# Half-step order of a joined scan-and-read stage, with the scan's normalised rows written by ScalarE

## The chip, the cores and the metric

The kernel runs on one core of one Trainium2 chip. The metric is the device time of one execution in microseconds. The kernel before has a median of 6312.4 us over three runs (6304.77 to 6313.58). In the text, a time is in us unless marked ns.

## The reference, cut to what matters

A network of four layers acts on x of shape 4 x 512 x 64 x 64 in float32. The change touches only the first, a test-time-training linear layer with 8 heads of 64 channels. The 4096 tokens of an image go through a scan in chunks of 16:

```python
def step(carry, inp):
    W1c, b1c = carry
    xq, xk, xv, et = inp
    Z1 = xk @ W1c + b1c
    grad = _ln_l2_bwd(Z1, xv - xk, g, bb)
    Attn1 = jnp.tril(xq @ xk.swapaxes(-1, -2))
    b1_bar = b1c - jnp.tril(et) @ grad
    Z1_bar = xq @ W1c - et * Attn1 @ grad + b1_bar
    last_eta = et[..., -1, :, None]
    W1n = W1c - (last_eta * xk).swapaxes(-1, -2) @ grad
    b1n = b1c - (last_eta * grad).sum(-2, keepdims=True)
    return ((W1n, b1n), xq + _ln(Z1_bar, g, bb, EPS_IN))
...
return _ln(out, post_w, post_b, EPS_IN) @ o_w.T
```

`_ln_l2_bwd` normalises Z1 (the normalised rows are `xh`) and returns the gradient of a squared error. The state W1, b1 goes from chunk to chunk, so the scan is one long chain. The outputs (Z1_bar, its norm, the post norm and the last projection) are off that chain.

## The kernel before

The program runs one stage after another: channel statistics, the projection of queries, keys and values, then the function `scan_and_read`, then a Fourier layer, a gate and a second Fourier layer. Only `scan_and_read` is changed. It joins two jobs.

The scan has 256 steps, one for each chunk of 16 tokens, of all four images at once. The images are in two groups of two (`g` 0 and 1). For each group a step is: `project_k` (TensorE: the bias sum and 16 small matmuls with the state into `ps_z`), `spread` (ScalarE: squares with their sums, then the root), `gradients` (VectorE: `zg`, the reciprocal `rstd`, the normalised rows `xh`, `t_row`, `tx`, `cx`, `core`, and `step`; GpSimd makes the rates, `b_step`, `b_sum` and `stored`), `update` (TensorE: the state in PSUM, `ps_w`), and `state_out` (ScalarE: the state from PSUM to SBUF for the next `project_k`). In the first step of each 8 the state is copied to `w_snap` in place of `w_sb`, and is kept there for the reads.

The read works on tiles of 128 tokens of one image, one tile for each two steps, through a pipeline: a tile is turned and weighted in slot KQ (4 slots after its own), summed in OUT (5), normalised in NORM (6), projected in PROJ (7) and leaves in LEAVE (8). One slot is two steps: an even one (`at.odd` 0) and an odd one. I call such a pair of steps a period; there are 128.

Each engine has its own queue, and its order of work is written out by hand in a function `body`. A step is cut into half steps: work of group 0, tile work, work of group 1, tile work. TensorE's order is `project_k(0)`, tile work, `update(1)` of the step before, tile work, `project_k(1)`, tile work, `update(0)`, tile work. In the even step its tile work is `tile_bias_and_state`, `tile_outputs_turn`, `tile_weighted` and the first of four `tile_project` parts; in the odd step `tile_query_turn`, `tile_project` 1, 2 and 3, `tile_weights` and `turn_keys`. ScalarE's order in the even step is `spread(0)`, `keys_out`, `normed`, `state_out(1)`, `outputs_turned`, `spread(1)`, `squares`, `state_out(0)`; in the odd step `spread(0)`, `head_roots`, `query_turned`, `output_squares`, `state_out(1)`, `spread(1)`, `output_root`, `state_out(0)`. VectorE's order in the even step is `gradients(0)`, `leave`, `gradients(1)`, `head_sums`, `outputs`, `moments`; in the odd step `gradients(0)`, `head_norms`, `variance`, `gradients(1)`, `shift_of`, `weights`. Waits on semaphores, counted by steps and tiles, tie the queues together; SyncE issues the transfers in its own order, the tile's rows of x (`x_sb`, line 1671) in the odd step of slot PROJ.

Of the kernel before, what the change touches and what calls it, by code (L numbers as in the profile page):

```python
# [13 lines left out]
P = 128  # L14
# [1385 lines left out]
def scan_and_read(nc, T, d, x_in, rec, q_in, grad, s_snap, x_out, chan_stats):  # L1400
# [14 lines left out]
    with ExitStack() as ctx:  # L1415
# [60 lines left out]
        x_sb = sb("x_in", [P, CT, P])  # L1476
# [50 lines left out]
        xh_sb = sig("xh_sb")  # L1527
# [9 lines left out]
        state_sb = sig("state_sb")  # L1537

# [3 lines left out]
        x_loaded = one("x_loaded", 16)  # L1542
# [63 lines left out]
        def state_of(g, at):  # L1606

            return w_snap[g][at.p] if at.c == 0 else w_sb[g]

        @block.sync  # L1610
        def _(sp):
# [36 lines left out]
            def body(at, scan):  # L1648
# [12 lines left out]
                if at.odd:  # L1661
                    tile = at.tile(LEAVE)
                    if tile:
                        t, b, sc, _ = tile
                        sp.wait_ge(y_done.sem, y_done.at(t, 1))
                        sp.dma_start(o_view[b, :, :, bass.ds(sc * P, P)], y_sb[b % 2][:]).then_inc(y_gone[b % 2].sem, 16)
                    tile = at.tile(PROJ)
                    if tile:
                        t, b, sc, _ = tile

                        sp.dma_start(x_sb[:], x_view[b, :, :, bass.ds(sc * P, P)]).then_inc(x_loaded.sem, 16)
# [47 lines left out]
        def _(pool):  # L1719
# [29 lines left out]
            def gained(tile):  # L1749
                t, b, sc, _ = tile  # L1750
                pool.wait_ge(zn_sb.sem, zn_sb.at(t, 1))
                pool.wait_ge(o_done.sem, o_done.at(t, 0))
                v.tensor_tensor(zgain[:], zn[:], read_gain[:].rearrange("p (h e) -> p h e", h=NH), ALU.mult).then_inc(zgain_sb.sem, 1)
# [7 lines left out]
            def body(at, scan):  # L1761
                if scan:
                    gradients(at, 0)
                if not at.odd and at.tile(NORM):
                    gained(at.tile(NORM))
# [8 lines left out]
        def _(act):  # L1774
            a = nc.scalar

# [41 lines left out]
            def squares(tile):  # L1818
                t, b, sc, _ = tile

                act.wait_ge(zn_sb.sem, zn_sb.at(t, 0))
                for n in range(2):
                    act.wait_ge(out_ps.sem, out_ps.at(t, n + 1))
                    a.copy(zo[:].rearrange("p (a n) e -> p a n e", n=2)[:, :, n], ps_out[n][:, :, 0:HD]).then_inc(zo_sb.sem, 1)
                act.wait_ge(hsq_sb.sem, hsq_sb.at(t, 0))
                act.wait_ge(zo_sb.sem, zo_sb.at(t, 2))
                a.activation(zsq[:], zo[:], ACT.Square).then_inc(zsq_sb.sem, 1)
# [25 lines left out]
            def body(at, scan):  # L1853
                kq, out, norm, proj = (at.tile(n) for n in (KQ, OUT, NORM, PROJ))
                following = Place(at.v, at.p, at.c + 1) if at.c < 7 else Place(at.v + at.p, 1 - at.p, 0)
                if scan:
                    spread(0, at.s)
                if not at.odd and (scan or at.slot == 0) and not (isinstance(at.s, int) and at.s == 0):

                    keys_out(at.v * 8 + at.slot + B - 1, at.p if at.c == 0 else 1 - at.p, (at.c // 2 - 1) % B)  # L1860
                if at.odd:
                    if out:
                        head_roots(out)
                    if kq:
                        query_turned(kq)
                    if norm:
                        output_squares(norm)
                elif proj:
                    normed(proj)
                if scan:  # L1870
                    state_out(1, at)
                if not at.odd and proj:
                    outputs_turned(proj)
                if scan:
                    spread(1, at.s)
                if at.odd:
                    if norm:
                        output_root(norm)
                elif out:
                    squares(out)  # L1880
                if scan:
                    state_out(0, following)
# [4 lines left out]
        def _(dve):  # L1887
# [34 lines left out]
            def gradients(at, g):  # L1922
# [12 lines left out]
                v.tensor_tensor(xh[g][:], z, wide(rstd[g][:]), ALU.mult).then_inc(xh_sb[g].sem, 1)  # L1935
# [4 lines left out]
                dve.wait_ge(xh_sb[g].sem, xh_sb[g].at(s, 1))  # L1940
# [18 lines left out]
            def leave(tile):  # L1959
# [3 lines left out]
                dve.wait_ge(x_loaded.sem, x_loaded.at(t, 16))  # L1963
                dve.wait_ge(y_gone[q].sem, y_gone[q].at(sc * 2 + b // 2, 0))
                dve.wait_ge(stats_sb.sem, stats_sb.at(t, 0))
                for n in range(CT):
                    done = v.scalar_tensor_tensor(y_sb[q][:, n], ps_y[:, n], T.wo_bias[:, n:n + 1], x_sb[:, n], ALU.add, ALU.add)  # L1967
# [9 lines left out]
            def outputs(tile):  # L1977
                t, b, sc, _ = tile
                dve.wait_ge(zgain_sb.sem, zgain_sb.at(t, 1))
# [3 lines left out]
                v.scalar_tensor_tensor(o_sb[:], zgain[:].rearrange("p h e -> p (h e)"), 1.0, qb[:].rearrange("p h e -> p (h e)"),  # L1983
# [28 lines left out]
            def head_norms(tile):  # L2012
# [5 lines left out]
                dve.wait_ge(zgain_sb.sem, zgain_sb.at(t, 0))  # L2018
                v.tensor_tensor(zn[:], zo[:], hrstd[:].unsqueeze(2).broadcast_to([P, NH, HD]), ALU.mult).then_inc(zn_sb.sem, 1)
# [9 lines left out]
            def body(at, scan):  # L2029
# [3 lines left out]
                if at.odd:  # L2033
                    if out:
                        head_norms(out)
                    if norm:
                        variance(norm)
                elif gone:
                    leave(gone)
                if scan:  # L2040
                    gradients(at, 1)
                if at.odd:
                    if norm:
                        shift_of(norm)
                    if kq:
                        weights(kq)
                else:
                    if out:
                        head_sums(out)
                    if norm:  # L2050
                        outputs(norm)
                    if gone:
                        moments(gone)
# [7 lines left out]
        def _(pe):  # L2061
# [47 lines left out]
            def tile_bias_and_state(tile):  # L2109
# [3 lines left out]
                pe.wait_ge(weigh_sb.sem, weigh_sb.at(t, 2))  # L2113
                out = [ps_out[n][:, :, 0:HD] for n in range(2)]
# [65 lines left out]
            def body(at, scan):  # L2180
# [6 lines left out]
                if at.odd:  # L2187
                    if kq:
                        tile_query_turn(kq, proj)
                    if proj:  # L2190
                        tile_project(proj, 1)
                elif out:
                    tile_bias_and_state(out)
                if update_last:
                    update(1, before)
                if at.odd:
                    if proj:
                        tile_project(proj, 2)
                elif proj:
                    tile_outputs_turn(proj)  # L2200
# [5 lines left out]
                elif out:  # L2206
                    tile_weighted(out)
                if scan:
                    update(0, at)
                if at.odd:  # L2210
                    if proj:
                        tile_project(proj, 3)
# [4 lines left out]
                elif proj:  # L2217
                    tile_project(proj, 0)
# [298 lines left out]
```

## Time and profile before

| | |
|---|---|
| median of the runs | 6312.4 us |
| the profiled execution's own time | 6306.89 us |
| its span | 6304.9 us |
| `scan_and_read`, first to last scan step in the trace | about 1720 to 4380 us |
| PE, DVE, ACT, POOL busy over the span | 87%, 65%, 36%, 38% |
| mean granted TensorE clock | 0.899 of full speed |

PE is TensorE, DVE is VectorE, ACT is ScalarE, POOL is GpSimd. PEclk 1.00 is 2.4 GHz and 0.50 is 1.2 GHz. In a timeline row the figures are the start and the duration in us of a run of equal instructions; `xN` counts them; a bracket gives the idle time of the engine before it and what ended it.

### The profile page before, as it was taken

What the parts mean: (1) busy time and instruction counts of PE and PEld (TensorE: products, weight loads), DVE (VectorE), ACT (ScalarE), POOL (GpSimd) and SP (SyncE); (2) the same over time, 40 slices, a digit from 0 to 9 for tenths busy, and PEclk for the clock granted to TensorE, in tenths of its full rate; (3) what the DMA queues carried; (4) which work ended last, traced back from release to release, by engine and by line L of the source; (5) the groups of instructions that cost most, each with busy time, mean ns of one, the idle gap of its engine ahead of it and who ended that gap; (6) DMA issues with size and microseconds to landing.
All of it is one profiled execution on the core that took longest, in us unless ns stands there. A gap on an engine that the chain in (4) does not pass through costs nothing. (4 is left out here: it accounts for less than half of the span.)

```text
span 6304.9 us, 141772 instructions
## 1 busy us (share of the span) xinstructions
PE 5494.0 (87%) x41532; PEld 3914.7 (62%) x41532; DVE 4074.0 (65%) x14538; ACT 2270.6 (36%) x6131; POOL 2390.9 (38%) x3910
## 2 busy tenths in 40 slices
PE   1799999999578889888888888888699999599999
PEld 0344444444267777777777777777566666377777
DVE  5566666566477777777777777777566666544444
ACT  0111111111155545555555555554233333233333
POOL 0244444444255544545545544544121222222222
PEclk9899999999778888888788878888899999799999
DMA  6233333333334444444444444444222211122221
GB/s 244 72 126 124 121 133 118 126 119 126 121 103 122 117 121 121 119 115 119 117 116 121 121 118 115 118 119 126 85 87 87 86 73 58 68 96 86 86 86 69
DMA packets 823322, 694.07 MB, mean 110 GB/s; under 512 B 357224, under 2 KB 758000, under 8 KB 811664
## 3 DMA queue, kind: packets, MB, share of 16 engines
q1 hardware_dynamic: 732304, 542.54, 28.9%
q10 hardware_dynamic: 90240, 142.75, 6.1%
q8 instruction: 293, 4.80, 0.3%
q14 instruction: 485, 3.97, 0.2%
HBM read 402.96 MB, written 282.20 MB: 109 GB/s over the span
## 5 line engine op out<-in xcount | busy, mean ns | idle before, releaser
L1390 PE MATMUL proj_ps<-proj_w_sb,proj_h 128*128 128x512 f32 x3072 | 1345.4, 596 | 0.0
L1390 PEld LDWEIGHTS proj_ps<-proj_w_sb,proj_h 128*128 128x128 f32 x3072 | 577.5, 190 | 742.9 <-issue 716.1
L2173 PE MATMUL scan_ps_y<-scan_o_t,proj_wo_sb 128*128 128x128 f32 x4096 | 631.0, 302 | 15.5 <-DVE scan_y L1967 14.8
L1312 DVE SCALAR_TENSOR_TENSOR proj_lin<-proj_ps,proj_rstd,proj_wbias_sb 128x512 f32<-128x512 f32 x384 | 284.4, 747 | 547.1 <-PE proj_ps L1390 546.1
L2173 PEld LDWEIGHTS scan_ps_y<-scan_o_t,proj_wo_sb 128*128 128x128 f32 x4096 | 547.1, 208 | 65.7 <-issue 26.0
L1736 POOL TENSOR_TENSOR scan_b_step<-scan_core,scan_rate_last 128x128 f32<-128x128 f32 x512 | 318.5, 622 | 640.0 <-DVE scan_core L1951 640.0
L2105 PE MATMUL scan_ps_w<-scan_step,scan_record 64*128 64x128 f32 x4088 | 430.0, 339 | 22.1 <-DVE scan_step L1956 21.8
L1787 ACT ACTIVATE scan_square<-scan_ps_z 128x64 f32<-128x64 f32 x1024 | 219.0, 219 | 569.5 <-PE scan_ps_z L2093 567.2
L1260 POOL TENSOR_TENSOR proj_by_cos<-proj_lin,proj_rope 128x512 f32<-128x512 f32 x256 | 340.1, 1338 | 138.9 <-DVE proj_lin L1312 109.4
L1266 POOL TENSOR_TENSOR proj_gk<-proj_rec,proj_gain_sb 128x256 f32<-128x256 f32 x256 | 181.1, 728 | 554.9 <-DVE proj_rec L1333 554.9
L2105 PEld LDWEIGHTS scan_ps_w<-scan_step,scan_record 64*128 64x128 f32 x4088 | 336.8, 230 | 56.5 <-DVE scan_step L1956 30.7
L266 POOL TENSOR_TENSOR fourier_spec<-fourier_prod 128x448 f32<-128x448 f32 (+1 forms) x80 | 93.1, 1164 | 704.9 <-DVE fourier_prod L410 704.8
L1780 ACT COPY scan_state_w<-scan_ps_w 128x512 f32<-128x512 f32 x448 | 259.2, 579 | 278.9 <-PE scan_ps_w L2105 273.7
L2117 PE MATMUL scan_ps_out<-scan_b_in,scan_ones 64*128 64x256 f32 x512 | 118.7, 549 | 276.4 <-DVE scan_weigh L2026 254.9
L2128 PE MATMUL scan_ps_out<-scan_grad_in,scan_weigh 128*128 128x64 f32 x2048 | 347.2, 340 | 0.0
L1728 POOL TENSOR_TENSOR scan_rate<-scan_rstd,scan_record 128x2 f32<-128x2 f32 x512 | 100.4, 196 | 649.0 <-DVE scan_rstd L1933 647.1
L2128 PEld LDWEIGHTS scan_ps_out<-scan_grad_in,scan_weigh 128*128 128x128 f32 x2048 | 328.0, 251 | 18.0 <-issue 14.1
L487 PE MATMUL fourier_psD<-fourier_mats,fourier_turned 128*128 128x128 f32 x2148 | 295.9, 282 | 42.1 <-DVE fourier_spec L389 39.6
L281 ACT COPY fourier_turned<-fourier_psT 128x512 f32<-128x512 f32 (+3 forms) x289 | 156.5, 550 | 488.7 <-PE fourier_psT L480 488.7
L487 PEld LDWEIGHTS fourier_psD<-fourier_mats,fourier_turned 128*128 128x128 f32 x2148 | 277.5, 197 | 86.6 <-issue 50.7
L706 POOL TENSOR_TENSOR fourier_spec<-fourier_prod 128x448 f32<-128x448 f32 (+1 forms) x80 | 86.4, 1080 | 618.8 <-DVE fourier_prod L799 618.8
L2087 PE MATMUL scan_ps_z<-scan_b_sum,scan_heads 128*32 128x128 f32 x4096 | 258.4, 331 | 46.2 <-issue 45.0
(287 smaller groups left out, 12263.8 us busy)
## 6 DMA issues: line engine op xcount, KB each, us to landing
scan_record<-records SPq DMA_DIRECT2D x1032, 98.0 KB
records<-proj_rec ACTq DMA_DIRECT2D x128, 784.0 KB, 3.6
scan_k_in<-records SPq DMA_DIRECT2D x266, 128.0 KB
spectra<-fourier_spec SPq DMA_DIRECT2D x16, 2112.0 KB, 6.4
fourier_spec<-spectra SPq DMA_DIRECT2D x16, 2112.0 KB, 8.2
stats_x<-x SPq DMA_DIRECT2D x16, 2048.0 KB, 7.8
proj_h<-x SPq DMA_DIRECT2D x32, 1024.0 KB, 7.1
queries<-proj_q ACTq DMA_DIRECT2D x128, 256.0 KB, 3.7
```

The costliest lines, as they stand in the source:

```text
L487: done = pe.matmul(psD[t % 2][:, col:col + P], turned[t % 2][:, j * P:(j + 1) * P], mat, start=True, stop=True)
L1260: g_.tensor_tensor(by_cos[q][:, n].rearrange("p (a e) -> p a e", e=32), lin[q][:, n].rearrange("p (a e) -> p a e", e=32), cos, ALU.mult).t ...
L1266: g_.tensor_tensor(by_parity(gk[q][:], n), keys(j, n), by_parity(T.gain[:], n), ALU.mult)
L1312: v.scalar_tensor_tensor(lin[q][:, n], ps[q][n][:], rstd[k][:, j:j + 1], T.wbias[:, n], ALU.mult, ALU.add).then_inc(lin_sb.sem, 1)
L1390: last = pe.matmul(ps[j % 2][n][:], h[k][:, ct, j * P:(j + 1) * P], T.w[:, n, ct], start=ct == 0, stop=ct == CT - 1)
L1736: v.tensor_tensor(b_step[g][:], core[g][:], rate_last[g][:, :, 2:3].broadcast_to([P, PB, HD]), ALU.mult).then_inc(b_step_sb[g].sem, 1)
L1780: a.copy(state_of(g, at)[:].rearrange("p r b a e -> p r (b a e)"), ps_w[:, :, g].rearrange("p r b a e -> p r (b a e)")).then_inc(state_sb[ ...
L1787: a.activation(square[:, g, b], ps_z[g][:, b * HD:(b + 1) * HD], ACT.Square, accum_out=ssq[g][:, b:b + 1]).then_inc(ssq_sb[g].sem, 1)
L2087: pe.matmul(ps_z[g][32 * a:32 * a + 32, 0:F], heads[:, 32 * a:32 * a + 32], b_sum[g][at.c % RING][:].rearrange("p b e -> p (b e)"), start= ...
L2105: done = pe.matmul(ps_w[:, r, g, b].rearrange("p a e -> p (a e)"), record[g][at.ring][rows, b, 0:2 * HD], step[g][rows, b].rearrange("p a ...
L2128: done = pe.matmul(ps_out[n][:, a, 0:HD], weigh[n][:, a], grad_sb[b % 2][:, 2 * a + n], start=False, stop=True, skip_group_check=True)
L2173: done = pe.matmul(ps_y[:, n], T.wo[:, ct, n * P:(n + 1) * P], o_t[:, ct], start=ct == 0, stop=ct == CT - 1)
```

## The change

- VectorE no longer makes `xh`. `spread` on ScalarE, after the root, waits for VectorE's reciprocal and makes `xh` with two activations (one for each image) that copy `ps_z` with a scale taken from `rstd`. VectorE waits for both before `tx`.
- The order of tile work changes on TensorE, ScalarE, VectorE and GpSimd.
- `w_snap[1]` is no longer written from PSUM but by a copy from `w_sb[1]` in the second step of each 8 (`keep_state`).
- The gain is multiplied before the norm of the heads, not after it; the number of operations stays.
- `x_sb` has two buffers, and its load is issued one slot earlier.

```diff
 state_of:   return w_snap[0][at.p] if g == 0 and at.c == 0 else w_sb[g]

 ScalarE
+            def keep_state(at, out):
+                sc = at.v * 2 + at.p
+                if out:
+                    act.wait_ge(out_ps.sem, out_ps.at(out[0], 2))
+                act.wait_ge(state_sb[1].sem, state_sb[1].at(at.s, 0))
+                a.copy(w_snap[1][at.p][:]..., w_sb[1][:]...).then_inc(kept_sb.sem, 1)
+                act.wait_ge(kept_sb.sem, kept_sb.at(sc, 1))
 spread:
                 a.activation(std[g][:], ssq[g][:], ACT.Sqrt, bias=eps[:]).then_inc(std_sb[g].sem, 1)
+                act.wait_ge(cx_sb[g].sem, cx_sb[g].at(s, 0))
+                act.wait_ge(rstd_sb[g].sem, rstd_sb[g].at(s, 1))
+                for b in range(PB):
+                    a.activation(xh[g][:, b], ps_z[g][:, b * HD:(b + 1) * HD], ACT.Copy, scale=rstd[g][:, b:b + 1]).then_inc(xh_sb[g].sem, 1)
 body, after:
                 spread(0); if even: keys_out
                 odd:  keep_state (second step of 8), outputs_out(out), output_squares(norm)
                 even: head_roots(norm)
                 state_out(1)
                 odd:  query_turned(kq)          even: normed(proj)
                 spread(1)
                 odd:  head_squares(out), output_root(norm)     even: outputs_turned(proj)
                 state_out(0)
...
 VectorE, gradients:
-                v.tensor_tensor(xh[g][:], z, wide(rstd[g][:]), ALU.mult).then_inc(xh_sb[g].sem, 1)
-                dve.wait_ge(xh_sb[g].sem, xh_sb[g].at(s, 1))
+                dve.wait_ge(xh_sb[g].sem, xh_sb[g].at(s, PB))
 body, after:
                 gradients(0)
                 odd:  variance(norm), moments(gone)            even: head_norms(norm), leave(gone)
                 gradients(1)
                 odd:  shift_of(norm), head_sums(out), weights(kq)     even: outputs(norm)
...
 TensorE, body, after:
                 project_k(0)
                 odd:  tile_query_turn(kq), tile_project(proj, 0)
                 update(1) of the step before
                 odd:  tile_project(proj, 1)                    even: tile_project(gone, 3)
                 project_k(1)
                 odd:  tile_weights(kq)                         even: tile_outputs_turn(proj), tile_bias_and_state(out)
                 update(0)
                 odd:  tile_project(proj, 2), turn_keys         even: tile_weighted(out)
...
 GpSimd: gained(out) in the odd step, between the groups; it reads zo
 SyncE:
-                    tile = at.tile(PROJ)
-                        sp.dma_start(x_sb[:], x_view[...]).then_inc(x_loaded.sem, 16)
+                    tile = at.tile(NORM)
+                        sp.dma_start(x_sb[b % 2][:], x_view[...]).then_inc(x_loaded[b % 2].sem, 16)
```

## Rows read from the trace of the kernel before

**Rows 1.** Busy us of each engine, 2200 to 4200 us, granted clock.
```profile
2200.00:4200.00 2000.00, 1746.67 (x21124) 1529.95 (x21122) 1536.97 (x7553) 1030.80 (x3394) 1004.05 (x2078) 0.81 0.45 118
```
**Rows 2.** Groups by line, 2200 to 4200 us: busy us, mean ns, idle before.
```profile
L2087 PE MATMUL scan_ps_z<-scan_b_sum,scan_heads 128*32 128x128 f32 x3016 | 189.7, 331 | 36.2 <-issue 36.2
L1935 DVE TENSOR_TENSOR scan_xh<-scan_ps_z,scan_rstd 128x128 f32<-128x128 f32 x378 | 110.1, 291 | 13.0
L1967 DVE SCALAR_TENSOR_TENSOR scan_y<-scan_ps_y,proj_wo_bias_sb,scan_x_in 128x128 f32<-128x128 f32 x377 | 106.1, 344 | 140.4 <-DMA scan_x_in<-x 139.7
```
**Rows 3.** Two stretches of 2 us, columns as in rows 1.
```profile
3026.00:3028.00 2.00, 0.40 (x4) 0.16 (x2) 1.75 (x13) 0.43 (x1) 0.60 (x3) 1.00 0.35 80
...
3032.00:3034.00 2.00, 2.00 (x18) 1.77 (x17) 0.00 (x0) 0.82 (x2) 0.00 (x0) 0.50 0.56 162
```
**Rows 4.** Timeline of VectorE, odd step from 3002.64, even step from 3011.33.
```profile
3000.26 0.68 DVE L1993 TENSOR_REDUCE scan_hsq<-scan_zsq 128x8 f32<-128x512 f32 x1
...
3001.86 0.87 DVE L1975 BATCH_NORM_STATS2 scan_stats<-scan_y 128x128 f32 x4
3002.64 0.27 DVE L1930 TENSOR_TENSOR scan_zg<-scan_ps_z,scan_gain 128x128 f32<-128x128 f32 x1
3002.84 0.15 DVE L1933 RECIPROCAL scan_rstd<-scan_std 128x2 f32<-128x2 f32 x1
3003.02 0.29 DVE L1935 TENSOR_TENSOR scan_xh<-scan_ps_z,scan_rstd 128x128 f32<-128x128 f32 x1
3003.23 0.47 DVE L1938 SCALAR_TENSOR_TENSOR scan_t_row<-scan_zg,scan_rstd,scan_record 128x64 f32<-128x64 f32 x2
...
3005.25 0.20 DVE L2016 RECIPROCAL scan_hrstd<-scan_hstd 128x8 f32<-128x8 f32 x1
...
3006.09 0.41 DVE L1999 TENSOR_TENSOR scan_ovar<-scan_nmean 128x1 f32<-128x1 f32 x1
...
3011.33 0.28 DVE L1930 TENSOR_TENSOR scan_zg<-scan_ps_z,scan_gain 128x128 f32<-128x128 f32 x1
```
**Rows 5.** Timeline of TensorE in the same even step, clock 1.00.
```profile
3011.47 0.70 PE L2117 MATMUL scan_ps_out<-scan_b_in,scan_ones 64*128 64x256 f32 x4 [2.90 <-DVE scan_weigh L2026]
...
3012.84 0.67 PE L2105 MATMUL scan_ps_w<-scan_step,scan_record 64*128 64x128 f32 x8
3013.44 0.66 PE L2137 MATMUL scan_ps_turn<-proj_ident_sb,scan_on 128*128 128x128 f32 x4
3014.02 0.42 PE L2087 MATMUL scan_ps_z<-scan_b_sum,scan_heads 128*32 128x128 f32 x8
3014.26 0.41 PE L2093 MATMUL scan_ps_z<-scan_state_w,scan_k_t 128*32 128x64 f32 x16
3014.60 2.00 PE L2128 MATMUL scan_ps_out<-scan_grad_in,scan_weigh 128*128 128x64 f32 x16
3016.53 0.72 PE L2105 MATMUL scan_ps_w<-scan_step,scan_record 64*128 64x128 f32 x8
```
**Rows 6.** Timeline of ScalarE around the same even step.
```profile
3009.18 0.30 ACT L1790 ACTIVATE scan_std<-scan_ssq,scan_eps 128x2 f32<-128x2 f32 x1
3009.39 1.24 ACT L1797 COPY scan_k_t<-scan_ps_turn 64x512 f32<-64x512 f32 x2
3010.65 0.81 ACT L1810 ACTIVATE scan_on<-scan_o,scan_oshift,scan_orstd 128x512 f32<-128x512 f32 x1
3013.55 0.58 ACT L1780 COPY scan_state_w<-scan_ps_w 128x512 f32<-128x512 f32 x1 [2.09 <-PE scan_ps_w L2105]
...
3014.74 0.22 ACT L1787 ACTIVATE scan_square<-scan_ps_z 128x64 f32<-128x64 f32 x1
```
**Rows 7.** Timeline of TensorE in an even step at clock 0.50.
```profile
3030.29 0.93 PE L2117 MATMUL scan_ps_out<-scan_b_in,scan_ones 64*128 64x256 f32 x4 [0.59 <-DVE scan_weigh L2026]
...
3032.61 1.18 PE L2105 MATMUL scan_ps_w<-scan_step,scan_record 64*128 64x128 f32 x8
...
3035.77 3.68 PE L2128 MATMUL scan_ps_out<-scan_grad_in,scan_weigh 128*128 128x64 f32 x16
```

More of the change, by code:

```diff
@@ L1537, in scan_and_read @@
         state_sb = sig("state_sb")
+        kept_sb = one("kept_sb")
         k_loaded = one("k_loaded", 32)
@@ L1541, in scan_and_read @@
         grad_in = [one(f"grad_loaded{q}", 48) for q in range(2)]
-        x_loaded = one("x_loaded", 16)
+        x_loaded = [one(f"x_loaded{q}", 16) for q in range(2)]
         y_gone = [one(f"y_gone{q}", 16) for q in range(2)]
@@ L1763, in body @@
                     gradients(at, 0)
-                if not at.odd and at.tile(NORM):
-                    gained(at.tile(NORM))
+                if at.odd and at.tile(OUT):
+                    gained(at.tile(OUT))
                 if scan:
@@ L1861, in body @@
                 if at.odd:
+                    if scan and at.c == 1:
+                        keep_state(at, out)
                     if out:
-                        head_roots(out)
+                        outputs_out(out)
+                    if norm:
+                        output_squares(norm)
+                elif norm:
+                    head_roots(norm)
+                if scan:
+                    state_out(1, at)
+                if at.odd:
                     if kq:
                         query_turned(kq)
-                    if norm:
-                        output_squares(norm)
                 elif proj:
@@ L1870, in body @@
                 if scan:
[L1871 to L1874, printed above, removed]
                     spread(1, at.s)
                 if at.odd:
+                    if out:
+                        head_squares(out)
                     if norm:
                         output_root(norm)
-                elif out:
-                    squares(out)
+                elif proj:
+                    outputs_turned(proj)
                 if scan:
@@ L2033, in body @@
                 if at.odd:
-                    if out:
-                        head_norms(out)
                     if norm:
                         variance(norm)
-                elif gone:
-                    leave(gone)
+                    if gone:
+                        moments(gone)
+                else:
+                    if norm:
+                        head_norms(norm)
+                    if gone:
+                        leave(gone)
                 if scan:
@@ L2044, in body @@
                         shift_of(norm)
+                    if out:
+                        head_sums(out)
                     if kq:
                         weights(kq)
[L2047 to L2053, printed above, removed]
+                elif norm:
+                    outputs(norm)
             loop(dve, body)
@@ L2190, in body @@
                     if proj:
-                        tile_project(proj, 1)
-                elif out:
-                    tile_bias_and_state(out)
+                        tile_project(proj, 0)
                 if update_last:
@@ L2197, in body @@
                     if proj:
-                        tile_project(proj, 2)
-                elif proj:
-                    tile_outputs_turn(proj)
+                        tile_project(proj, 1)
+                elif gone:
+                    tile_project(gone, 3)
                 if scan:
@@ L2205, in body @@
                         tile_weights(kq)
-                elif out:
-                    tile_weighted(out)
+                else:
+                    if proj:
+                        tile_outputs_turn(proj)
+                    if out:
+                        tile_bias_and_state(out)
                 if scan:
@@ L2216, in body @@
                         turn_keys(at.v * 8 + at.slot + B)
-                elif proj:
-                    tile_project(proj, 0)
+                elif out:
+                    tile_weighted(out)
             loop(pe, body)
```

40 lines of the change are left out of this document (24 added, 16 removed).

## The prediction

> **What bounds the kernel now.** I read the page's slices first: the joined stage holds some 2660 of 6305 us and is the only one that the change touches. Then the busy time in its steady part, 2200 to 4200 us [rows 1]: TensorE works 1747 of 2000 us, VectorE 1537, ScalarE 1031, GpSimd 1004, at a mean granted clock of 0.81. The `xh` instruction ran 378 times there [rows 2], four times for each pair of steps, so there were 94.5 periods and one lasts 21.16 us. Per period TensorE idles 2000 minus 1747, over 94.5, which is 2.68 us.
>
> The clock is the second half of the story. With only the two levels 1.00 and 0.50, a mean of 0.81 means 38% of the time at 1.2 GHz, 8.0 us of each period. The stretches show where: in 3026 to 3028 TensorE worked 0.40 of 2 us at 1.00, and in 3032 to 3034 it worked all the time and had 0.50 [rows 3]. So a wait of TensorE of some 3 us costs itself and then makes the work behind it slow.
>
> Third, the timelines show what TensorE waits for. It idled 2.90 us in the even step for VectorE's `weights` [rows 5], the last thing that VectorE does in the odd step. VectorE starts its next `zg` at 3011.33, 8.69 us after the odd step's `zg` at 3002.64, without a gap between [rows 4]. So in the odd half VectorE is the bound, and in the even half TensorE's queue is, the more so at 1.2 GHz: bias and state take 1.37 us at the high clock (3011.47 to 3012.84, [rows 5]) and 2.32 at the low one (3030.29 to 3032.61, [rows 7]).
>
> **The change part by part.**
>
> *`xh` on ScalarE.* VectorE saves 0.21 us a time (3003.02 to 3003.23, [rows 4]). But `tx` needs `xh`. No row of before shows an activation of this form, so I bound it. From below: the square of the same 128x64 shape, without scale, lasts 0.22 [rows 6]. From above: the root, 0.30, whose next instruction starts 0.21 later, plus 64 columns. `on` takes a scale and a bias from SBUF and lasts 0.81, against 0.58 for a plain copy of the same 512 columns [rows 6], so such an operand costs about 0.1. I take 0.31 each, 0.22 apart. Then `xh` is ready 0.20 (reciprocal and its signal) + 0.22 + 0.31 + 0.04 = 0.77 us after the reciprocal starts; without the old `xh`, VectorE has its `t_row` pair behind it after 0.18 + 0.39 = 0.57. It waits 0.20 and saves 0.21: nothing. At the lower bound it saves 0.2 a time, 0.8 per period.
>
> The Trainium skill, page "ScalarE: Activation LUTs", section "What ACT_TABLE_LOAD costs", says that each per-partition pointer operand adds about 93 ns; the 0.81 against 0.58 for two of them agrees roughly. The same page's "Rules for kernel authors" tell to do a multiply on VectorE and not on ScalarE, which speaks against this edit. By the page's figures one `xh` would be 0.33 us as an estimate, and the sum would come out 0.1 us per period higher than mine.
>
> *ScalarE now waits for VectorE.* This is the costly part. The reciprocal of group 0 in the even step stands in VectorE's queue behind all of the odd step. Behind the waiting `xh` on ScalarE stand `keys_out`, `head_roots`, `state_out(1)`, and for that last one TensorE's `project_k(1)` waits. Before, ScalarE ran ahead: `keys_out` at 3009.39 and `on` at 3010.65 were done before VectorE began at 3011.33 [rows 4, 6].
>
> *The order of VectorE.* The odd half loses `head_norms`, 0.84 (3005.25 to 3006.09), and takes `moments`, 0.78, and `head_sums`, 0.60 (its 0.68 less the overlap of 0.08 that neighbours have) [rows 4]. It becomes 8.69 - 0.84 + 0.78 + 0.60 = 9.23 us.
>
> *One period at the high clock, from `zg(0)` of the odd step at 0.* The even reciprocal starts at 9.23 + 0.20 = 9.43. ScalarE is past `xh` 0.20 + 0.44 later (10.07), past `keys_out` at 11.33 (1.26, 3009.39 to 3010.65), past `head_roots` at 11.54 (0.21, as the root), and starts `state_out(1)`. The state product follows 0.71 later (3013.55 to 3014.26, [rows 5, 6]): 12.25. `normed` starts at 12.11 and ends at 12.92; `tile_outputs_turn` begins at 12.97. Then TensorE has turn 0.58, bias and state 1.37, update 0.65 (0.72 less overlap), weighted 1.93, bias sum 0.24 [rows 5], and the odd state product starts at 17.74. To its square are 0.48 (3014.26 to 3014.74), to the root and `zg` another 0.54: the next odd `zg` is at 18.76. VectorE isn't the bound in the even half, and TensorE's own odd work (8 to 9 us) fits into VectorE's 9.23 and then idles some 3.4 us before 12.25. The old order has nothing like it: at the high clock its period was 18.77 in the timeline with a wait of 1.3 for x, so 17.5 without.
>
> *The low clock.* TensorE's wait is longer than the 2.68 us of today, so the clock should fall as often, just when the even chain starts. Before, 8.0 us of a period run low; some of them reach into the odd half, where the new order has slack, so I let 7.3 us fall behind 12.25, to 19.55. Turn then takes 1.1 (scaled like its neighbours), bias and state 2.32, update 1.11, and weighted 3.61 [rows 7]. Turn starts at 12.97, weighted at 17.50, of which 2.05 of 3.61 are done by 19.55; the rest takes 0.83 at the high clock. With 0.24 and 1.02 the next `zg` is at 21.64. To this I add the idle time in front of the bias sum that no engine releases, 36.2 us in 94.5 periods or 0.38 [rows 2], which stays. The same working for the old order (chain from the end of `weights`) gives 20.4 + 0.38 = 20.8 against 21.16 measured, the rest being waits for x.
>
> *`keep_state`.* A copy of 0.58 [rows 6] once in four periods ahead of `state_out(1)`: with its waits 0.1 per period at most, nothing if VectorE hides it. I take 0.1.
>
> *x a slot earlier.* VectorE waits 139.7 us for x in 94.5 periods, 1.48 each [rows 2]. The wait goes: the load has 20 us more. Behind it now stands the even TensorE chain, so nothing is gained beyond what is in the period above. The other SyncE issues keep their order and number. GpSimd's `gained` moves to the odd half, where GpSimd (50% busy) is free. These edits I cost at nothing.
>
> *Sum.* 21.64 + 0.38 + 0.1 = 22.1 us against 21.16, +0.93 per period. 124 of the 128 periods have tile work: +115 us. The profiled execution took 6306.9, so 6422; the median of the runs is 5.5 higher: 6427, about 1.8% slower. I say 6425.
>
> **The rivals.**
>
> *A: the even half is shorter than I work out, and VectorE's relief and the missing x wait count (faster).* Place: between VectorE's even reciprocal and `project_k(1)`. If ScalarE's chain there were 1.2 us shorter and `xh` at its lower bound, TensorE's wait would fall to about 1.7 us per period, 1.0 under today's, and with it the slow work behind it. That is 1 us per period, 124 us: 6190. For it: the page shows ScalarE just half busy, and x waits are real. Against: the chain's terms are read from rows one by one.
>
> *B: the clock stays high (faster).* Then a period is 18.76 + 0.48 = 19.2, 1.9 less than now: -240 us, 6070. It decides when TensorE's idle pieces become too short for the clock to fall. Against: my schedule has the longer piece.
>
> The Trainium skill, page "TensorE: Matmul & The Clock Gate", section "HAM oscillation — how this bites in real kernels", describes the same thing: waits between groups of matmuls bring the slow clock back each time. By it the trace agrees [rows 3].
>
> *C: nothing measurable.* The longer even chain and the waits taken away cancel: 6300 to 6325.
>
> *D: worse (slower).* The low clock reaches through the odd half too; TensorE, now with `tile_project` 0 ahead of `update(1)` there, makes VectorE late: 1.5 us more in half of the periods, some 100 us on top: 6530.
>
> **How the numbers follow.** The forecast case (6330 to 6500) has 0.55, A 0.22, B 0.08, C 0.06, D 0.09. What a measurement can tell from no change is about 0.2%, 13 us. So faster 0.30, same 0.06, slower 0.64. The range for 8 in 10 must reach into A, whose centre is 6190, and into D: 6190 to 6545. The forecast's own range is 6330 to 6500.
>
> **What would show it.** In the changed profile: (1) periods of about 22 us from 2200 us on; (2) ScalarE's `xh` idle before it on VectorE's reciprocal, above all in even steps; (3) TensorE's wait of about 3 us now before the state product of group 1 in the even step, released by the state copy, and none for `weights`; (4) a mean clock of about 0.8; (5) no wait of VectorE for x, but one of 1 to 4 us before `zg(0)` in the odd step; (6) `gradients` no shorter than 2.6 us. It is wrong if TensorE idles less than 2 us per period or if the clock is above 0.9.

## The result, and the profile after

The changed kernel takes 6646.8 us (median of four runs, 6643.7 to 6654.2), the kernel before on the same chip 6308.7 (6304.8 to 6313.6): a ratio of 1.054 with a 95% interval of 1.052 to 1.056. It is 5.4% slower. The forecast was 6425, slower by 1.8%, with 6190 to 6545 as its range: the sign was right, the size was not, and the time lies 100 us outside the range.

From the page after: the head, the engines' busy time, and the granted clock in the 40 slices.

```profile
span 6646.0 us, 144036 instructions
...
PE 5796.6 (87%) x41532; PEld 4159.8 (63%) x41532; DVE 3997.7 (60%) x14026; ACT 2489.2 (37%) x7187; POOL 2385.9 (36%) x3910
...
PEclk9899999999567777777777777777889999799999
```

Each digit of the last line is the granted clock in tenths over a fortieth of the span. The joined stage holds the eleventh digit to the twenty-ninth; it starts with 5 and 6, ends with 8, and all digits between are 7. From the first `zg` to the last it takes 3033 us, for 2657 before: 376 more, of which 35 are made good by a shorter rest of the program. In its steady part, with the columns of [rows 1]:

```profile
2200.00:4200.00 2000.00, 1736.96 (x18559) 1509.88 (x18557) 1296.23 (x6287) 1043.47 (x3660) 880.70 (x1819) 0.72 0.39 104
```

TensorE is as busy as before (1737 against 1747 us) and did less: 18,559 matmuls against 21,124. That is the mark of a clock loss. A clock of 0.72 means 56% of the time at 1.2 GHz, against 38% before.

The groups by line of the same 2000 us (count, then busy us and mean ns, then the engine's idle us before it and what ended that):

```profile
L1954 DVE TENSOR_TENSOR scan_zg<-scan_ps_z,scan_gain 128x128 f32<-128x128 f32 x331 | 94.1, 284 | 537.4 <-ACT scan_square L1798 537.3
L1990 DVE SCALAR_TENSOR_TENSOR scan_y<-scan_ps_y,proj_wo_bias_sb,scan_x_in 128x128 f32<-128x128 f32 x329 | 92.1, 341 | 0.0
...
L1805 ACT ACTIVATE scan_xh<-scan_ps_z,scan_rstd 128x64 f32<-128x64 f32 x662 | 172.5, 310 | 188.8 <-DVE scan_rstd L1957 188.8
```

`zg` ran 331 times, four to a period: 82.75 periods of 24.17 us, where 94.5 periods of 21.16 stood. VectorE's wait for x is gone (0.0 against 139.7 in [rows 2]), but VectorE now waits 537 us for the squares of the next group, that is, for TensorE's state products.

The waits by pairs in the same stretch (released <- releaser: sum us, count, longest):

```profile
DVE scan_zg L1954 <- ACT scan_square L1798: 537.3, 173, 5.6
PE scan_ps_z L2117 <- ACT scan_state_w L1791: 180.5, 82, 2.9
PE scan_ps_z L2111 <- ACT scan_k_t L1812: 35.8, 21, 2.2
```

The second row is TensorE's wait that the prediction worked out: 82 times in 82.75 periods. The third is the same wait in one period of four, where the bias sum needs the new keys too and the wait is split in two. Here is a whole one, TensorE's timeline (start, duration, engine, line; in brackets the idle time before and what ended it):

```profile
3040.74 0.43 PE L2111 MATMUL scan_ps_z<-scan_b_sum,scan_heads 128*32 128x128 f32 x8
...
3044.03 0.53 PE L2117 MATMUL scan_ps_z<-scan_state_w,scan_k_t 128*32 128x64 f32 x16 [2.86 <-ACT scan_state_w L1791]
...
3044.84 1.11 PE L2163 MATMUL scan_ps_turn<-proj_ident_sb,scan_on 128*128 128x128 f32 x4 [0.28 <-ACT scan_on L1825]
3045.88 1.23 PE L2143 MATMUL scan_ps_out<-scan_b_in,scan_ones 64*128 64x256 f32 x4
3046.90 1.81 PE L2147 MATMUL scan_ps_out<-scan_state_snap,scan_q_t 64*128 64x64 f32 x16
3048.50 1.17 PE L2129 MATMUL scan_ps_w<-scan_step,scan_record 64*128 64x128 f32 x8
3049.60 3.67 PE L2154 MATMUL scan_ps_out<-scan_grad_in,scan_weigh 128*128 128x64 f32 x16
3053.63 0.65 PE L2117 MATMUL scan_ps_z<-scan_state_w,scan_k_t 128*32 128x64 f32 x16
```

Behind the wait each instruction takes 1.8 times its time of [rows 5]: bias 1.23 for 0.70, weighted 3.67 for 2.00. The chain from ScalarE's side, which makes the wait:

```profile
3041.41 0.52 ACT L1805 ACTIVATE scan_xh<-scan_ps_z,scan_rstd 128x64 f32<-128x64 f32 x2 [1.42 <-DVE scan_rstd L1957]
3041.82 1.22 ACT L1812 COPY scan_k_t<-scan_ps_turn 64x512 f32<-64x512 f32 x2
3043.07 0.30 ACT L1858 ACTIVATE scan_hstd<-scan_hsq,scan_read_eps 128x8 f32<-128x8 f32 x1
3043.39 0.58 ACT L1791 COPY scan_state_w<-scan_ps_w 128x512 f32<-128x512 f32 x1
```

ScalarE stands idle 1.42 us at `xh` until VectorE's reciprocal; `keys_out`, the head roots and the state copy go one by one behind it, and TensorE starts as the copy ends its work. VectorE around the same point:

```profile
3030.15 0.29 DVE L1954 TENSOR_TENSOR scan_zg<-scan_ps_z,scan_gain 128x128 f32<-128x128 f32 x1 [5.38 <-ACT scan_square L1798]
...
3036.00 0.29 DVE L1954 TENSOR_TENSOR scan_zg<-scan_ps_z,scan_gain 128x128 f32<-128x128 f32 x1 [1.25 <-ACT scan_square L1798]
...
3040.97 0.28 DVE L1954 TENSOR_TENSOR scan_zg<-scan_ps_z,scan_gain 128x128 f32<-128x128 f32 x1
3041.17 0.15 DVE L1957 RECIPROCAL scan_rstd<-scan_std 128x2 f32<-128x2 f32 x1
...
3042.06 0.22 DVE L1966 SCALAR_TENSOR_TENSOR scan_tx<-scan_t_row,scan_xh 128x64 f32<-128x64 f32 x1 [0.20 <-ACT scan_xh L1805]
...
3054.90 0.29 DVE L1954 TENSOR_TENSOR scan_zg<-scan_ps_z,scan_gain 128x128 f32<-128x128 f32 x1 [5.56 <-ACT scan_square L1798]
```

And the clock, in 2 us stretches (columns of [rows 1]):

```profile
3042.00:3044.00 2.00, 0.00 (x0) 0.00 (x0) 1.69 (x12) 1.93 (x5) 0.56 (x1) 1.00 0.42 99
3044.00:3046.00 2.00, 1.69 (x22) 1.13 (x22) 1.97 (x8) 1.43 (x6) 1.23 (x3) 0.55 0.83 214
...
3052.00:3054.00 2.00, 2.00 (x30) 1.85 (x30) 0.00 (x0) 0.00 (x0) 0.00 (x0) 0.50 0.65 167
...
3056.00:3058.00 2.00, 2.00 (x13) 1.68 (x12) 1.65 (x11) 1.17 (x5) 0.49 (x2) 0.53 0.47 150
3058.00:3060.00 2.00, 2.00 (x38) 1.76 (x38) 1.25 (x6) 1.24 (x4) 1.76 (x4) 1.00 0.76 210
```

The clock is at 1.00 until the wait ends, falls as the even chain begins, stays at 0.50 through all of it, and is back near 3058, some 3 us into the odd half. Such stretches, from 2200 to 3400 us, after: 50 in about 50 periods, 42 of them 13.6 us long, mean 13.3. Before: 50 in about 57 periods, mean 9.1, of mixed length (19 of 6.8 us, 9 of 3.4, the rest 10.2 to 17). So the clock falls hardly oftener per microsecond; it stays down longer, and at the same place in each period.

### The profile page after: what moved, and what is told of

Its sections match the earlier page's. It is cut to its first block and busy times, and to the rows that moved or that the text cites. A ratio compares the mean times of both kernels' runs of the same rounds, so it can differ in the third digit from the quotient of the medians.

```text
span 6646.0 us, 144036 instructions
## 1 busy us (share of the span) xinstructions
PE 5796.6 (87%) x41532; PEld 4159.8 (63%) x41532; DVE 3997.7 (60%) x14026; ACT 2489.2 (37%) x7187; POOL 2385.9 (36%) x3910
## 5 line engine op out<-in xcount | busy, mean ns | idle before, releaser
L2199 PE MATMUL scan_ps_y<-scan_o_t,proj_wo_sb 128*128 128x128 f32 x4096 | 675.4, 317 | 1.6 <-DVE scan_y L1990 0.9
L1954 DVE TENSOR_TENSOR scan_zg<-scan_ps_z,scan_gain 128x128 f32<-128x128 f32 x512 | 145.7, 285 | 825.8 <-ACT scan_square L1798 825.5
L2199 PEld LDWEIGHTS scan_ps_y<-scan_o_t,proj_wo_sb 128*128 128x128 f32 x4096 | 597.5, 224 | 47.3 <-ACT scan_o_t L1831 2.0
L2117 PE MATMUL scan_ps_z<-scan_state_w,scan_k_t 128*32 128x64 f32 x7680 | 256.4, 268 | 288.2 <-ACT scan_state_w L1791 287.4
L2154 PE MATMUL scan_ps_out<-scan_grad_in,scan_weigh 128*128 128x64 f32 x2048 | 461.8, 419 | 0.0
L2154 PEld LDWEIGHTS scan_ps_out<-scan_grad_in,scan_weigh 128*128 128x128 f32 x2048 | 438.0, 325 | 27.9 <-issue 27.6
L1791 ACT COPY scan_state_w<-scan_ps_w 128x512 f32<-128x512 f32 x480 | 280.5, 584 | 383.6 <-PE scan_ps_w L2129 380.3
L2117 PEld LDWEIGHTS scan_ps_z<-scan_state_w,scan_k_t 128*32 128x32 f32 x7680 | 206.0, 139 | 334.7 <-ACT scan_state_w L1791 330.7
L1805 ACT ACTIVATE scan_xh<-scan_ps_z,scan_rstd 128x64 f32<-128x64 f32 x1024 | 266.8, 310 | 289.4 <-DVE scan_rstd L1957 289.4
L266 POOL TENSOR_TENSOR fourier_spec<-fourier_prod 128x448 f32<-128x448 f32 (+1 forms) x80 | 86.7, 1083 | 697.5 <-DVE fourier_prod L410 697.5
```

Of the source, the lines that this page charges most:

```text
L1791: a.copy(state_of(g, at)[:].rearrange("p r b a e -> p r (b a e)"), ps_w[:, :, g].rearrange("p r b a e -> p r (b a e)")).then_inc(state_sb[ ...
L1805: a.activation(xh[g][:, b], ps_z[g][:, b * HD:(b + 1) * HD], ACT.Copy, scale=rstd[g][:, b:b + 1]).then_inc(xh_sb[g].sem, 1)
L2117: done = pe.matmul(ps_z[g][32 * a:32 * a + 32, b * HD:(b + 1) * HD], k_t[q][PB * g + b][:, a, CS * at.c:CS * at.c + CS].rearrange("p t n - ...
L2154: done = pe.matmul(ps_out[n][:, a, 0:HD], weigh[n][:, a], grad_sb[b % 2][:, 2 * a + n], start=False, stop=True, skip_group_check=True)
L2199: done = pe.matmul(ps_y[:, n], T.wo[:, ct, n * P:(n + 1) * P], o_t[:, ct], start=ct == 0, stop=ct == CT - 1)
```

## The experiments

The theory: `xh` on ScalarE in the new order makes the wait before the state product of group 1, and that wait brings 13.5 us of low clock, which is most of the loss. Rivals: the new order is slow by itself; the idle time matters and the clock only goes with it; something else, such as SyncE's queue, bounds it. A ratio below is to the kernel before on the same chip: 6314.4 for the first four, 6293.6 for the next four, 6318.6 for the last two. Periods and clock are from 2200 to 4200 us.

**1. The order alone.** The changed kernel with `xh` back on VectorE.

```
-  for b in range(PB):   # ScalarE, spread
-      a.activation(xh[g][:, b], ps_z[g][...], ACT.Copy, scale=rstd[g][:, b:b + 1])
+  v.tensor_tensor(xh[g][:], z, wide(rstd[g][:]), ALU.mult)   # VectorE, gradients
```

> The changed kernel with xh back on VectorE, so only the new order of tile work (and the rest of the change) is left. Theory (ScalarE, which now waits for VectorE's even reciprocal before keys_out and state_out(1), makes TensorE's one long wait): the wait before the state product of group 1 in the even step falls from about 2.7 us to 1 us or less, VectorE becomes the bound with a period of 17.5 to 19.5 us against 24.2, and the time is 6000 to 6150 us. Rival (the new order alone is the cause, TensorE's even chain of turn, bias, state, update and weighted without slack): the period stays at 22 us or more and the time at 6450 to 6650.

Measured 6256.5 (6251.6 to 6268.5), ratio 0.992 (0.989 to 0.994): the order is not slow, it is 0.8% faster than before. The whole loss hangs on the place of `xh`. The time is 107 us above the expected span and the period is 21.0 us, for the 17.5 to 19.5 expected. The stretch and the waits say why:

```profile
2200.00:4200.00 2000.00, 1641.75 (x21324) 1422.71 (x21324) 1520.99 (x7620) 1021.11 (x3444) 1018.15 (x2096) 0.88 0.45 120
```

```profile
PE scan_ps_turn L2177 <- DMA scan_q_in<-queries: 178.3, 80, 6.2
PE scan_ps_z L2114 <- ACT scan_state_w L1791: 69.8, 83, 1.3
```

The wait for the state copy fell from 180.5 us to 69.8, and the longest from 2.9 to 1.3. In its place TensorE waits 178.3 us for the query tile. All in all it idles 358 of 2000 us here, against 263 in the changed kernel, and yet the kernel is 390 us faster, at a clock of 0.88 for 0.72: the sum of the idle time is not what the loss goes by. In the timelines of TensorE and of SyncE's queue:

```profile
3005.68 1.12 PE L2177 MATMUL scan_ps_turn<-proj_ident_sb,scan_q_in 128*128 128x128 f32 x4 [2.87 <-DMA scan_q_in<-queries]
```

```profile
3002.95 0.36 SPq L1633 DMA_DIRECT2D scan_q_in<-queries  x1
```

The load is issued 2.73 us before the turn that needs it. It is late because it is issued late: from 2200 to 4200 us SyncE's queue shows not one wait in this run, it only issues. In the changed kernel, whose period is longer, it waits for its work:

```profile
SPq L1677 <- POOL scan_stored L1747: 401.2, 200, 3.6
```

(SyncE's queue waits for the rows that GpSimd writes in `stored`, before it issues their transfer.)

**2. `xh` alone.** The kernel before with only `xh` moved, the edit of experiment 1 the other way round.

> The kernel before, with xh made by two ScalarE activations and nothing else changed. Theory (ScalarE's wait hurts by what stands behind it and is needed by TensorE): in the old order update(1) comes late in the even step, some 2 us after VectorE's reciprocal, so the wait mostly hides: 6310 to 6430 us. Rival (the move of xh costs the same wherever it is put): 6550 us or more. Second rival (it relieves VectorE, which bounds the odd half): below 6290.

Measured 6402.2 (6391.1 to 6429.0), ratio 1.016 (1.012 to 1.019), a clock of 0.79 and periods of 22.0 us, within the first expected span.

```profile
2200.00:4200.00 2000.00, 1728.86 (x20346) 1502.89 (x20345) 1453.28 (x6903) 1153.39 (x3994) 945.59 (x1997) 0.79 0.43 114
```

So the order alone gives -0.8%, `xh` alone +1.6%, both +5.4%. They don't add up: their product would be +0.7%. `xh` costs 88 us in the old order and 390 in the new one (6646.8 less 6256.5, each on its own chip, whose kernels before differ by 6 us). In both orders `state_out(1)` stands behind the waiting `xh`. What differs is TensorE's `update(1)`, whose result that copy takes. In the old order it stands behind `tile_bias_and_state`, which waits for `weights`, and so comes late by itself; TensorE hardly waits for the copy:

```profile
PE scan_ps_z L2096 <- ACT scan_state_w L1780: 22.9, 33, 1.1
```

In the new order `update(1)` is done early (3039.01 to 3039.73 in the step shown above), and the copy, at 3043.39, is held by ScalarE's queue alone: 180.5 us of waits.

**3. A shorter queue behind `xh`.** The changed kernel with `keys_out` (1.22 us) moved behind `state_out(1)`.

```
-  keys_out(...)            # behind spread(0)
   ...
   state_out(1, at)
+  keys_out(...)
```

> The changed kernel with keys_out on ScalarE put behind state_out(1). TensorE's total idle time per period should stay about 3 us, because tile_outputs_turn still waits for keys_out and normed, but it is cut into two pieces, about 1.4 us before the state product and about 1.5 us before the turn. Theory (the low clock follows from one long piece of idle time): the stretches at 1.2 GHz get fewer or shorter than 13.5 us per period, and the time is 6300 to 6550 us. Rival (the total idle time counts, however it is cut): clock and time as in the changed kernel, 6620 to 6680.

Measured 6571.1 (6563.2 to 6573.7), ratio 1.041 (1.039 to 1.043).

```profile
PE scan_ps_turn L2163 <- ACT scan_on L1825: 107.4, 74, 1.7
PE scan_ps_z L2117 <- ACT scan_state_w L1791: 94.5, 73, 1.5
```

```profile
2200.00:4200.00 2000.00, 1714.16 (x19024) 1495.10 (x19020) 1332.97 (x6447) 1063.06 (x3750) 904.96 (x1868) 0.75 0.40 106
```

The wait for the state copy halved as `keys_out` left, which shows that the queue makes it. But 107 us of waits for `on` came (the turn stands behind the same ScalarE queue), and the sum of TensorE's idle time did not fall: 286 us, 3.4 per period of 23.6, for 3.2. Only 76 us of the 338 came back. The time is 21 us above the expected span and 49 under the rival's, so neither was right. The wait for the copy fell from 2.9 to 1.5 us at most and that for `on` is 1.7 at most, but the clock rose only from 0.72 to 0.75: from 2200 to 4200 us 54 of 85 low stretches still lasted 13.6 us, mean 11.7. Two such waits close together bring nearly what one of 2.9 us brings.

**4. The wait filled.** The changed kernel with eight unread matmuls ahead of `project_k(1)` in even steps. They write a part of PSUM that nobody reads; they are work added.

```
   tile_project(gone, 3)
+  if scan:
+      for _ in range(8):
+          pe.matmul(ps_z[1][:, 256:384], T.ident[:], T.ident[:], start=True, stop=True, ...)
```

> The changed kernel with 8 matmuls of 128 columns, whose results nobody reads, in TensorE's queue ahead of project_k(1) in the even step, where it idles some 2.7 us. Theory (the low clock behind the wait costs more than the wait itself): the granted clock in the stage rises from 0.72 to 0.95 or more, the period falls from 24.2 to about 19.2 us, and the time is 6000 to 6150 us though work was added. Rival (the clock is not the cause, the chain of waits is): no gain, 6640 to 6800 us.

Measured 6247.4 (6243.2 to 6250.7), ratio 0.990 (0.988 to 0.992): 399 us less than the changed kernel, with some 2 us of work more per period.

```profile
3022.97 1.95 PE L2227 MATMUL scan_ps_z<-proj_ident_sb 128*128 128x128 f32 x16
```

```profile
2200.00:4200.00 2000.00, 1761.91 (x23056) 1543.37 (x23055) 1519.61 (x7305) 1204.02 (x4252) 1021.94 (x2114) 0.93 0.45 120
```

The filler removes nothing from ScalarE's or VectorE's chain; it only keeps TensorE at work in the wait. The clock went from 0.72 to 0.93 and the period from 24.2 to 20.8. This is the test that parts the theory from its rival: had the chain of waits been the price and the clock only its companion, no microsecond could have come back. The time is 97 us above the expected span; waits of up to 5.4 us for queries stayed, and experiment 8 shows what they and the late keys were worth.

**5. The same filler in the kernel before**, ahead of `tile_bias_and_state` in even steps, where TensorE waited 2.90 us in [rows 5].

```
+  pe.wait_ge(t_sb[1].sem, ...)      # the step before has read ps_z[1]
+  pe.wait_ge(xh_sb[1].sem, ...)
+  for _ in range(8):
+      pe.matmul(ps_z[1][:, 256:384], T.ident[:], T.ident[:], start=True, stop=True, ...)
   tile_bias_and_state(out)
```

> The kernel before, with 8 matmuls of 128 columns, whose results nobody reads, in TensorE's queue ahead of tile_bias_and_state in the even step, where it idles some 2.7 us for VectorE's weights. Theory (the low clock behind a long wait costs more than the wait, in the old order too): the clock in the stage rises from 0.81 to 0.93 or more, the period falls from 21.2 to about 19.2 us (VectorE's 17.5 and its wait for x), 6030 to 6150 us. Rival (only the changed kernel suffers from the clock): 6290 to 6330 us.

Measured 6235.1 (6230.1 to 6238.0), ratio 0.992 (0.989 to 0.994).

```profile
2200.00:4200.00 2000.00, 1747.05 (x23328) 1534.04 (x23330) 1568.08 (x7779) 1063.00 (x3499) 1047.64 (x2139) 0.96 0.46 122
```

```profile
DVE scan_y L1967 <- DMA scan_x_in<-x: 238.1, 86, 7.3
```

The clock half of the theory holds (0.81 to 0.96), the time half does not, by 85 us, nor does the rival: VectorE's wait for x grew from 139.7 us to 238.1. The kernel before had a second bound close under the first, the late load of x; SyncE's queue, which issues it, shows no wait in this run, as in experiment 1. Here the clock was worth 59 us, in the changed kernel 399.

**6. Three fillers in place of eight** in the changed kernel.

> As e4_filled_wait, but with 3 of the matmuls in place of 8, so the even step's wait falls from about 2.7 to about 1.8 us and no further. Theory (how long TensorE idles in one piece decides how long the low clock lasts): the stretches at 1.2 GHz become shorter than 13.5 us, as in the kernel before after waits of 1.4 to 2 us, and the time is 6350 to 6550 us, between the changed kernel and e4. Rival (any idle piece at that place brings the full stretch): 6600 to 6680 us.

Measured 6463.2 (6442.8 to 6476.6), ratio 1.029 (1.025 to 1.032), as expected.

```profile
2200.00:4200.00 2000.00, 1747.36 (x20529) 1520.21 (x20528) 1405.35 (x6768) 1115.54 (x3941) 947.61 (x1961) 0.82 0.42 112
```

```profile
PE scan_ps_z L2117 <- ACT scan_state_w L1791: 158.1, 98, 2.2
```

None, three, eight: 6647, 6463, 6247 us; clock 0.72, 0.82, 0.93; longest wait for the state copy 2.9, 2.2, 1.1. From 2200 to 3400 us the clock fell 50, 37 and 18 times, for 13.3, 11.0 and 8.4 us on the mean. In this row both the number and the mean length of the falls go down with the filled part of the wait. The theory's wording, that the longest wait decides the length, does not hold beyond it: experiment 3 had long falls behind waits of 1.7 us, and in the kernel before falls of 3.4 us followed waits of 1.2 to 3.2 us, falls of 13.6 waits of 1.8 to 3.5.

**7. The late loads taken off SyncE.** Experiment 1 (`xh` on VectorE) with the loads of queries and keys issued by ScalarE in even steps.

```
-  load_query(t, b, sc)                       # SyncE, odd step
-  load_keys(b, v * 2 + n)
+  loads(at, kq, scan)                        # ScalarE, even step, act.dma_start(...)
   spread(1, at.s)
```

> e1_order_only (new order, xh on VectorE) with the loads of the queries and keys issued by ScalarE in the even step in place of SyncE at the end of the odd step. Theory (in e1 SyncE's queue of 24 issues per period became the bound, seen as TensorE's wait of 1.9 us per period for the queries): that wait goes, the clock rises from 0.88 above 0.93, the period falls from 21.0 to 18.5 to 19.5 us, 5950 to 6080 us. Rival (the wait moves on to the records or gradients, which still stand in SyncE's queue): 6200 to 6260 us.

Measured 6076.0 (6069.0 to 6086.3), ratio 0.966 (0.963 to 0.969), as expected. The wait for queries is all but gone (4.2 us in five times); the largest left is for the bias load:

```profile
PE scan_ps_out L2143 <- DMA scan_b_in<-sum_snapshots: 121.7, 31, 8.1
```

```profile
2275.35 0.70 PE L2143 MATMUL scan_ps_out<-scan_b_in,scan_ones 64*128 64x256 f32 x4
...
2291.84 0.70 PE L2143 MATMUL scan_ps_out<-scan_b_in,scan_ones 64*128 64x256 f32 x4
...
2336.67 1.22 PE L2143 MATMUL scan_ps_out<-scan_b_in,scan_ones 64*128 64x256 f32 x4 [8.10 <-DMA scan_b_in<-sum_snapshots]
```

An undisturbed period takes 16.5 us, the mean 19.6.

**8. Experiment 4 with those loads on ScalarE**, `xh` there too.

> e4_filled_wait (changed kernel with 8 filling matmuls) with the same loads issued by ScalarE. Theory: e4 waits only 0.45 us per period for the queries, and ScalarE now stands in the chain, so the gain is small or nothing: 6180 to 6270 us. Rival (SyncE's lateness is what holds e4 at 20.8 us a period): 6050 to 6150 us.

Measured 6139.0 (6126.9 to 6176.9), ratio 0.977 (0.972 to 0.982). The rival was right: the loads gain 108 us here too (6247.4 to 6139.0, each on its own chip; to the kernel before, 0.990 to 0.977). With the clock at 0.95, `xh` on ScalarE costs 63 us against experiment 7, filler included.

**9. Two more DMAs off SyncE.** Experiment 7 with the load of x and the store of y issued by ScalarE at the end of odd steps.

```
-  sp.dma_start(o_view[...], y_sb[b % 2][:])      # SyncE
-  sp.dma_start(x_sb[b % 2][:], x_view[...])
   state_out(0, following)                        # ScalarE
+  act.dma_start(o_view[...], y_sb[b % 2][:])
+  act.dma_start(x_sb[b % 2][:], x_view[...])
```

> e7_loads_on_act with the load of x and the store of y issued by ScalarE too, at the end of the odd step. Theory (in e7 SyncE, with 21 issues per period, is still the bound, seen as waits of up to 8 us for b_in at the first step of each 8): these waits shrink from 122 us in 2000, the period falls from 19.6 to 18.5 to 19.2 us, 5960 to 6040 us. Rival (the waits at the first step of each 8 come from the landing of the gradients and not from SyncE's queue): 6060 to 6100 us.

Measured 6013.8 (5999.0 to 6023.9), ratio 0.952 (0.949 to 0.955), as expected. The stage ends at 4105 us here; until then a period lasts 18.8 us, for 19.6. It is the best of all kernels here.

```profile
PE scan_ps_out L2142 <- DMA scan_b_in<-sum_snapshots: 57.6, 31, 5.7
```

**10. The changed kernel with the loads on ScalarE**, no filler: does the loss shrink when SyncE is relieved?

> The changed kernel (xh on ScalarE, no filling) with the loads of queries and keys issued by ScalarE, to be compared with e7, which differs only in where xh is made. Theory (xh on ScalarE costs through ScalarE's wait for VectorE's reciprocal, TensorE's long wait and the low clock, whatever SyncE does): 6580 to 6700 us, some 550 us above e7. Rival (SyncE's queue has a part in the changed kernel's time): 6400 us or less.

Measured 6647.3 (6644.7 to 6654.1), ratio 1.052 (1.050 to 1.055), as expected.

```profile
2200.00:4200.00 2000.00, 1739.36 (x18403) 1511.48 (x18402) 1289.56 (x6248) 1037.57 (x3632) 878.47 (x1809) 0.72 0.39 103
```

Nothing moved against the changed kernel. So SyncE has no part in its loss. Against experiment 7 the place of `xh` alone is worth 571 us (6647.3 less 6076.0; the kernels before of the two chips differ by 25 us). Relieving SyncE pays only where the wait behind `xh` is gone.

## Why the prediction was right in sign and wrong in size

- **`xh` on ScalarE costs VectorE nothing: right.** 0.31 each and 0.52 for the pair were measured, 0.31 and 0.53 (0.22 + 0.31) used; VectorE waits 0.20 for it where it saves 0.21, and from `zg` to the work behind `gradients` it takes 2.75 us (3040.97 to 3043.72), for 2.61 before. The Trainium skill, page "ScalarE: Activation LUTs", section "What ACT_TABLE_LOAD costs", gives about 93 ns per pointer operand, by which I had estimated 0.33 us; the trace has 310 ns, a little under it.
- **ScalarE waits for VectorE, and TensorE for the state copy: right.** From the even reciprocal the state product was put at 2.82 us (12.25 less 9.43) and came at 2.86 (3041.17 to 3044.03); the turn at 3.54 and came at 3.67.
- **The odd half at the high clock, 9.23 us: too short, with what follows below.** From `zg(0)` to `zg(0)` it took 10.82 in the rows shown: VectorE waited 1.25 us in it for TensorE, whose work at its start ran at 1.2 GHz, and 0.33 for a result of its own. The mean of 82 periods is 10.3.
- **TensorE idles some 3.4 us before 12.25: a little too long.** It was 2.86 in this step; idle time of all kinds is 263 us in 82.75 periods, 3.18 us each, for 3.4 and 0.38 in the sum.
- **"The low clock": this step failed.** It carried over the 8.0 us of before and let 7.3 of them fall behind 12.25. Measured are 56% of 24.17, 13.5 us per period. The price per microsecond was nearly right: the forecast went from 19.24 (18.76 + 0.48) to 22.1 on 7.3 us, 0.39 us each. No run has this order at the high clock throughout, but between runs the price is 0.37 (from the changed kernel to experiment 1: 3.2 us of period for 8.5 of low clock) and 0.32 (to experiment 4: 3.4 for 10.6). The length of the stretch was the mis-sized term, and nothing in the argument had worked it out: it was carried over from the order of before, as if it came with each wait, whatever the order. In the order of before the waits differed from period to period (2.90 us in [rows 5], 0.59 in [rows 7]) and falls were of 3.4 to 17 us; the new order repeats one long wait at one place, and 42 of 50 falls are 13.6 us. The missing 2 us per period lie half in each place that the forecast kept at the high clock: 10.3 for 9.23 us in the odd half, and 13.9 for 12.9 from there on, where the end of the even chain (weighted 3.67 us, bias sum and state product) ran at 1.2 GHz too.
- **Rival D had the mechanism and was given 0.09.** The low clock does reach into the odd half, some 3 us, and VectorE does wait there for TensorE (`zg` of group 1, 1.25 us). It was priced at 1.5 us in half of the periods, 0.75 each; measured is 0.77 each on the mean, over 0.5 in 74 of 82. So D's size was right too, and its 6530 is still 117 us short, since the rest of the miss is in the even chain.
- **`keep_state`, x a slot earlier: no sign against their costs.** No wait for x is left. No run has one of these edits alone; with the new order, and without `xh`, they cost nothing (experiment 1). Rivals A and B fall: TensorE's wait did not fall under that of before, and the clock did not stay high. Experiments 1 and 4 show what each of the two would have needed: `xh` off ScalarE, or a filled wait.
- **The signs named.** Periods 24.2 for 22; ScalarE's idle before `xh` 188.8 us, there; the wait for the state copy, there; clock 0.72 for 0.8; x gone and the wait before `zg(0)` there, but 5.4 and 5.6 us in the rows shown, for the 1 to 4 that were named; `gradients` not under 2.6.

The Trainium skill, page "TensorE: Matmul & The Clock Gate", section "HAM oscillation — how this bites in real kernels", says that idle gaps between groups of matmuls bring the slow clock back again and again. The trace agrees (50 falls in 1200 us), with gaps of 2.86 us, shorter than the 3 to 5 us of the page's example. Experiments 4 and 6 add that filling the gap takes most of the falls away.

Shown: that the loss comes from the place of `xh` in this order (1, 7 and 10), through the wait behind it on ScalarE (3, 6), and that most of it is clock (4, 6). Open: why one wait costs 13.6 us of low clock and others less. Filling the wait lowers number and mean length of the falls, but neither the longest wait (3) nor the sum of the idle time (1) gives them by itself; the runs do not show the rule.

## What to carry to other kernels

Before an operation moves to a half-idle engine, list what is queued behind it there, what it will wait for, and which other engine waits for the last of the list; a cheap instruction that joins two chains can cost their whole sum. Price a wait of TensorE by the slow work that follows it, for the full chain behind it, and don't carry over the low-clock share of a different order. Where the clock is the loss, a few unread matmuls in the wait are a quick test of it; where it goes away and the time stays, as in experiment 5, read which wait has taken its place.

## What the runs showed of the hardware that was not expected

- More work in less time: sixteen matmul records of 1.95 us together, read by nobody, made the changed kernel 6.0% faster (6646.8 to 6247.4) and the kernel before 0.9% faster (6293.6 to 6235.1).
- Work that follows a wait of 2.86 us ran at 1.2 GHz for 13.6 us, although TensorE idles only 3.18 us in 24.17. With more idle time (3.8 us in 21.0, experiment 1) the clock was higher, 0.88 for 0.72; with the wait cut in two (experiment 3) it was hardly so, 0.75.
- Issuing DMAs was a bound of its own. SyncE's queue shows no wait in experiment 1, it only issues. An issue there lasts 0.36 us for a query tile; a pair for the bias lasts 1.41 in experiment 7:

```profile
2332.85 1.41 SPq L1693 DMA_DIRECT2D scan_b_in<-sum_snapshots  x2
```

  With two kinds of load and then two more issues moved to ScalarE, the kernel went from 6256.5 to 6076.0 and 6013.8 us.
